# Item sums in 8 local slots per tile and a third picked tile in a message-passing kernel

## The reference

```python
v = edge_attr * (KS - 1); lo = jnp.floor(v); f = v - lo        # KS = 4, three dimensions
idx = jnp.clip(lo[:, None, :] + bits[None], 0, KS - 1)         # 8 corners of 64 = 4*4*4 cells
basis = jnp.prod(jnp.where(bits[None] == 1, f[:, None, :], 1.0 - f[:, None, :]), axis=-1)
wi = idx[..., 0] + KS * idx[..., 1] + KS * KS * idx[..., 2]
z = jnp.einsum('nc,kco->nko', x, W)                            # W is 64 x 32 x 32
msg = sum over the 8 corners s of basis[:, s, None] * z[src, wi[:, s]]
agg = segment_sum(msg, dst) / clip(count of dst, 1)[:, None]
return agg + x @ R + b
```

## Time and profile before

| | us |
|---|---|
| median of 3 runs | 20,975.38 |
| lowest, highest | 20,951.05, 21,013.64 |
| span of the profiled execution | 20,957.9 |
| TensorE busy (share of the span) | 15,299.0 (73%) |
| VectorE busy | 11,387.0 (54%) |
| GpSimd busy | 11,380.3 (54%) |
| ScalarE busy | 3,304.1 (16%) |

### The profile page before, as it was taken

The page is one execution under the profiler, slowest core; times in us unless marked ns, Lnnn a source line. Parts: engine busy times, 40 slices in busy tenths (PEclk is TensorE's granted clock), DMA queues, the critical chain, the costliest instruction groups (busy, mean ns, idle before and its releaser), DMA issues.

```text
span 20957.9 us, 179979 instructions
## 1 busy us (share of the span) xinstructions
PE 15299.0 (73%) x55111; PEld 8212.8 (39%) x55111; DVE 11387.0 (54%) x19145; ACT 3304.1 (16%) x4009; POOL 11380.3 (54%) x12003
## 2 busy tenths in 40 slices
PE   7788888888866767676666676667666676766676
PEld 3333333333333444443433343444443343434343
DVE  4556666656655555555545555555555555555555
ACT  1111111111111111111111111111111111111111
POOL 5445555555545555555545555555554555555554
PEclk7666666666678888888878888888887888888888
DMA  1000000000010000000010000000001000000000
GB/s 33 13 14 15 15 15 15 15 14 15 15 24 16 16 16 16 16 16 16 16 23 16 17 16 16 16 16 16 17 16 23 16 16 16 16 16 16 16 16 22
DMA packets 886190, 353.06 MB, mean 17 GB/s; under 512 B 604191, under 2 KB 877680, under 8 KB 885872
## 3 DMA queue, kind: packets, MB, share of 16 engines
q0 software_dynamic: 386208, 210.78, 5.9%
q1 hardware_dynamic: 329276, 112.29, 2.3%
q10 hardware_dynamic: 170644, 29.29, 0.8%
HBM read 314.88 MB, written 36.56 MB: 17 GB/s over the span
## 4 chain that ended last, share of the span: by engine, by line
PE 51%; another core or an unknown queue 28%; issue 14%; ACT 3%; DVE 3%; ACTq 1%; DMA 0%; POOL 0%; DVEq 0%; SPq 0%; POOLq 0%
PE ps L1547 17%; PE ps L1559 16%; PE ps L1459 5%; PE ps L1570 4%; PE ps L1475 3%; ACT big L792 2%; PE ps L1448 2%; PE ps L1442 2%; DVE big L1056 1%; PE ps L1432 1%; ACT big L710 1%; ACTq L802 1%; ACT big L700 0%; PE ps L1414 0%
## 5 line engine op out<-in xcount | busy, mean ns | idle before, releaser
L571 POOL DMA_INDIRECT xg<-x_rows,idx x8790 | 8316.4, 946 | 6310.6 <-DVE big L1254 3682.7
L1547 PE MATMUL ps<-big 128*128 128x256 f32 x18816 | 5050.5, 422 | 1286.7 <-ACT big L792 1250.4
L1237 DVE TENSOR_TENSOR big<-ps,onehot 128x1024 f32<-128x1024 f32 x2352 | 2864.7, 1218 | 5084.9 <-remote 3417.8
L1547 PEld LDWEIGHTS ps<-big 128*128 128x128 f32 x18816 | 3863.2, 211 | 3111.9 <-issue 2581.3
L571 POOL DMA_INDIRECT xg<-in_x,idx x3125 | 2974.6, 952 | 2806.5 <-DVE big L1026 1826.0
L1570 PE MATMUL ps<-big,w_taps 128*32 128x512 f32 x9408 | 1544.9, 734 | 3060.8 <-issue 2851.8
L792 ACT COPY big<-ps 128x1024 f32<-128x1024 f32 x2352 | 2353.5, 1013 | 8828.4 <-PE ps L1547 5318.7
L1559 PE MATMUL ps<-xw,big 128*128 128x512 f32 x8232 | 3671.5, 597 | 50.5 <-issue 23.2
L1459 PE MATMUL ps<-w,big 65*128 65x256 f32 x6272 | 2498.1, 541 | 126.9 <-DVE big L1056 85.6
L1559 PEld LDWEIGHTS ps<-xw,big 128*128 128x128 f32 x8232 | 1543.4, 190 | 2006.9 <-issue 1981.1
L1459 PEld LDWEIGHTS ps<-w,big 65*128 65x128 f32 x6272 | 1566.0, 267 | 1875.0 <-issue 1562.7
(11 more groups left out here) (139 smaller groups left out, 6620.8 us busy)
## 6 DMA issues: line engine op xcount, KB each, us to landing
xg<-x_rows,idx POOLq DMA_INDIRECT x8790
xg<-in_x,idx POOLq DMA_INDIRECT x3125
row_of<-pick_rows SPq DMA_DIRECT2D x294, 128.0 KB
agg_rows<-rts ACTq DMA_DIRECT2D x294, 64.0 KB
meta<-in_coord_t SPq DMA_DIRECT2D x294, 48.0 KB
big<-in_rad SPq DMA_DIRECT2D x196, 64.0 KB
meta<-meta_items SPq DMA_DIRECT2D x392, 32.0 KB
idx<-in_src_t SPq DMA_DIRECT2D x392, 16.0 KB
```

The source lines that it names most:

```text
L571: return nc.gpsimd.indirect_dma_start(out=dst_tile, out_offset=None, in_=table, in_offset=bass.IndirectOffsetOnAxis(ap=index, axis=0))
L1237: v.tensor_tensor(bm[:, ring], hat_outer[:, its].rearrange("p n c b -> p n (c b)").unsqueeze(3) .to_broadcast([P, 4, 16, J]), onehot[:, it ...
L1547: tr = nc.tensor.matmul(ps[:, 2 * (ch % 2) + r // 2, 256 * (r % 2):256 * (r % 2) + 256], xm[:, at].rearrange("p a c -> p (a c)"), bm[:, at ...
```

## The change

In the narrow path of the three layers a tile now has LOCAL = 8 local slots, which begin at its first destination rounded down to an even number (PAIR = 2). The widest tile of these inputs reaches place 7 there; the branch to the wide path now asks for 8 or more. Item sums have 128 columns instead of 256, taps 256 instead of 512, and `S` and `onehot` are half as wide. A chunk is 8 tiles, so a step has 4 chunks, one per group; `bm` and `xm` are rings of four such chunks, which is a whole step. GpSimd's group q waits for `xm_ready[q]`.

The frames of the scan are those of before (16 slots from a multiple of 8). So before the scan VectorE shifts each tile's 8 sums to their place in the frame: a one-hot of the shift (0, 2, 4 or 6), a product with it into four shifted copies (`spread`, whose other slots stay zero), and a sum over these (`in_pairs_to_frame`). The scan then reads `summed` in SBUF, not `ps`. It stands after the second of four chunks, before after the third of eight. The shift comes with `carry` as a second row.

PICKS = (1, 2, 3): the last tile of three groups is picked, so GpSimd has 29 gathers in groups of 8, 7, 7 and 7. The nodes of the seventh block of `xw` are 212, so that a short product (64 columns, L1659) with a table of their own, `tail`, takes the place of the seventh wide one; SyncE loads `tail` once per layer. The places come ready from a table, so `slot` (L1204) is dropped in the narrow path.

The diff, cut to its core (the tables' preparation and the wide path's side are left out):

```diff
+LOCAL = 8
+PAIR = 2
+SHIFTS = HALF // PAIR
...
-PICKS = (1, 3)
+PICKS = (1,2,3)
...
+        def layer_of(path):
+
+            tiles = 4 * J // path.slots
+            S, at = part(0, (2, 16, STEP, path.slots))
+            bm, at = part(at, (4, tiles, 16, path.slots))
+            xm, at = part(at, (4, tiles, GROUP, CH))
...
-                            else lambda q: (xm_ready[2 * q + 1], l * STEPS + i - 1))
+                            else lambda q: (xm_ready[(q + 1) * chunks // 4 - 1], l * STEPS + i - 1))
...
+            def in_pairs_to_frame(par, at):
+
+                v.tensor_tensor(layer.hot_shift, carry[:, par, 1].unsqueeze(1).to_broadcast([P, SHIFTS, STEP]),
+                                slot_ids[:, 0:SHIFTS].unsqueeze(2).to_broadcast([P, SHIFTS, STEP]), ALU.is_equal
+                                ).then_inc(dve_step, 1)
+                dve.wait_ge(dve_step, at + 1)
+                v.tensor_tensor(layer.spread[:, :, 0:LOCAL, :],
+                                ps[:, 7, 0:LOCAL * STEP].rearrange("p (s i) -> p s i", s=LOCAL).unsqueeze(1)
+                                .to_broadcast([P, SHIFTS, LOCAL, STEP]),
+                                layer.hot_shift.unsqueeze(2).to_broadcast([P, SHIFTS, LOCAL, STEP]), ALU.mult
+                                ).then_inc(dve_step, 1)
+                dve.wait_ge(dve_step, at + 2)
+                reach = (J - PAIR) * STEP
+                v.tensor_reduce(layer.summed.rearrange("p s i -> p (s i)")[:, 0:reach],
+                                layer.spread.rearrange("p d s i -> p (d s i)")[:, 0:SHIFTS * reach]
+                                .rearrange("p (d x) -> p x d", d=SHIFTS), AX.X, ALU.add).then_inc(dve_step, 1)
...
-                for ch in range(8):
-                    its = slice(4 * ch, 4 * ch + 4)
-                    ring = slice(4 * (ch % 4), 4 * (ch % 4) + 4)
-
-                    if due(8 * n1 + ch - 3):
-                        dve.wait_ge(s_done[ch % 4], 2 * n1 + ch // 4)
+                tiles = layer.tiles
+                for ch in range(layer.chunks):
+                    its = slice(tiles * ch, tiles * ch + tiles)
+                    q, last_of = (tiles * ch) // QUART, (tiles * (ch + 1)) % QUART == 0
+
+                    if due(layer.chunks * n1 + ch - 3):
+                        dve.wait_ge(s_done[ch % 4], each * n1 + ch // 4)
...
-                    if ch == 2 and with_scan:
-                        scan(n - 2, prior + LINKS1, P, l + 1, par, twice - 2)
+                    if ch == SCAN_AT and with_scan:
+                        scan(n - 2, prior + 7, P, l + 1, par, twice - 2)
...
-                for r in range(4):
-                    at = 4 * (ch % 4) + r
-                    tr = nc.tensor.matmul(ps[:, 2 * (ch % 2) + r // 2, 256 * (r % 2):256 * (r % 2) + 256],
-                                          xm[:, at].rearrange("p a c -> p (a c)"),
-                                          bm[:, at].rearrange("p k s -> p (k s)"), start=True, stop=True)
+                for r in range(tiles):
+                    at = wide * (r % (tiles // 2))
+                    tr = nc.tensor.matmul(ps[:, 2 * (ch % 2) + r // (tiles // 2), at:at + wide],
+                                          layer.xm[:, ch % 4, r].rearrange("p a c -> p (a c)"),
+                                          layer.bm[:, ch % 4, r].rearrange("p k s -> p (k s)"), start=True, stop=True)
...
-                for b in range(WB):
-                    tr = nc.tensor.matmul(ps[:, 6, :], row_hot[:, k, b, :], xw[:, b, :], start=(b == 0),
-                                          stop=(b == WB - 1))
-                tr.then_inc(pick_done, 1)
+                if k == 0:
+                    pe.wait_ge(pick_in, 48 + 16 * (l + 1))
+                for b in range(WB - 1):
+                    nc.tensor.matmul(ps[:, 6, :], row_hot[:, k, b, :], xw[:, b, :], start=(b == 0),
+                                     stop=False)
+                nc.tensor.matmul(ps[:, 6, 0:TAIL * CH], row_hot[:, k, WB - 1, :], tail[:], start=False,
+                                 stop=True).then_inc(pick_done, 1)
```

More of the change, by code:

```diff
@@ L49 @@
 BANK = 512
-Path = namedtuple("Path", "narrow items steps blocks picks")
+Path = namedtuple("Path", "narrow items steps blocks picks slots")
 def sizes(nodes, edges):
@@ L78, in graph_kernel @@
     LAYERS = 3
+    FULL = (WB - 1) * P * J
+    TAIL = 1
+    while TAIL * P < nodes - FULL:
+        TAIL *= 2
     ds = bass.ds
@@ L780, in scalar_program @@
                 nc.scalar.copy(x1[:, b, :], xw[:, b, :]).then_inc(x1_ready, 1)
+            layer = layer_of(path)
             def l1_step(l, i, par, with_rows):
[L784 to L785 removed]
+                n, each = layer.tiles, layer.chunks // 4
+                for ch in range(layer.chunks):
+                    if ch == layer.chunks // 2 and with_rows:
                         l1_rows(l, i - 2)
@@ L1184, in vector_program @@
             link(v.reciprocal(rcnt[:], rcnt[:]))
-            LINKS1 = 8
+            SCAN_AT = 1 if path.narrow else 2
+            LINKS1 = 7 if path.narrow else 8
+            each = layer.chunks // 4
+            row_hot, picked = layer.row_hot, layer.picked
             def l1_step(l, i, par, twice, prior, with_scan):
@@ L1262, in vector_program @@
                 link(v.tensor_copy(rows_ps, window_ids[:]))
+                if path.narrow and l == 0:
+                    link(v.memset(layer.spread, 0.0))
+                    link(v.memset(layer.summed, 0.0))
                 base1 = steps[0]
-                per1 = LINKS1 + SCAN
+                per1 = LINKS1 + SCAN + SPREAD
                 for b in range(WB):
```

234 lines of the change are left out of this document (142 added, 92 removed).

## The result

| | before | after |
|---|---|---|
| median, us | 20,979.92 (4 runs) | 21,892.85 (4 runs) |
| lowest to highest | 20,951.05 to 21,013.64 | 21,810.04 to 21,945.05 |
| ratio, 95% interval | | 1.0438, 1.0409 to 1.0467 |
| span of the profiled execution | 20,957.9 | 21,922.1 |

The change is 4.4% slower; the forecast was 5% faster, and the time lies above its own range (to 20,370 us) and above the wider one (to 21,100). The page's chain has changed its shares: what stood under "an unknown queue" has mostly become "issue", time in which an engine waits for nothing that the profile shows.

The account below looks back on a forecast made before the run. GpSimd's gathers plus idle from late-seen TensorE completions bound a step: 36.2 + 7.8 + 2.0 = 46.0 us for 49.75; -3.75 x 288 = -1080, -15 elsewhere, gives 19,880 us. Own range 19,450 to 20,370, wider 19,000 to 21,100.

Parts of the forecast that it names:

- Chains, groups, pauses: GpSimd: 29 gathers a step in chains of 22 and 7, with idle about 8 and 2 us.
- Work of the engines: TensorE's work a step 26 us for 31, VectorE net +1.0 on 26.0 busy; gathers 36.2 us.
- the reduction: VectorE's sum of 1792 values before the scan: 1.9 to 3.6 us, taken as 2.7.
- The next first pick ends at 25.4, 13.9 us into group 2's chain: held: TensorE finishes this pick during the 22 gathers; VectorE sees its completion only after them, 4.07 us past the end.
- the 7.8 forecast: GpSimd's idle behind 22 gathers: 4.07 us of late release, first pick 1.73, `xm` 1.22, 0.8 to GpSimd.
- The sum of the range: The step's own range from the reduction, the tail and the cold pick: 44.5 to 47.7 us.
- the tail: Time from the last gather of a long chain to TensorE's completions becoming visible: 4.07 us, range 3.3 to 4.8.
- the cold pick: TensorE's second pick, slow after the release, may last 10 us instead of 5.35; +0.8 us in the range.
- Rival A: The third pick is also held beside a chain: two holds at full price, 51.8 us a step, 21,550 us; chance 0.14.
- hold: TensorE's completions become visible late while a long chain of gathers runs, the last 4.07 us after it.
- Rival C: Completions were late only from crowded ScalarE or TensorE queues; halved work frees them: 37.5 us a step, 17,430 us; chance 0.06.

Follow-up runs that it names:

- e4: The changed kernel with one gather per group in the layers, 4 a step instead of 29, results not the reference's: 16,027.2 us, ratio 0.7633.
- e5: The changed kernel with 8 of TensorE's 16 taps products moved behind the next step's first pick and first chunk: 20,411.0 us, ratio 0.9800 to the kernel before.
- e2: The kernel before with the third pick alone added, 16 slots and chunks of 4 tiles kept: 20,098.9 us, ratio 0.9575.
- e13: The changed kernel word for word, in a comparison without holds: 15,037.5 us against 15,372.7 for the kernel before.

## Why the prediction was wrong

- *Chains, groups, pauses.* Right: 22 and 7, pauses of 1.8 for 2.0 us, the long idle before the first pick, none before `bm`.
- *Work of the engines.* Right in size: item sums 16 records in 2.05 us (what the forecast counts as 64 products are the two records each of 32), a pick 5.6 (5.35 forecast), the reduction 3.26 (2.7), VectorE 28.2 us busy a step for 27.0 forecast, and none of it is the bound (e4: 32.9 us).
- *"The next first pick ends at 25.4, 13.9 us into group 2's chain: held".* This step failed. It took TensorE to work on through a chain, with only its completions seen late. In fact its records come 1.5 to 2.8 us apart once a chain of this kernel is some 10 us old, and the taps were first in its queue. So all records of the pick but one came after the chain, and its 12 wide ones, 5.3 to 5.4 us elsewhere in the step, took 9.4 us here and 7.5 in the next step, at granted clocks of 0.68 and 0.69. The idle is 14.7 us in the mean for the 7.8 forecast, +7 x 288 = 2,000 us, the distance from 19,880 to 21,893. e5 puts the pick ahead of the taps, and the mean idle is 8.2.
- *What misled.* In the step I read, completions are late but TensorE doesn't creep. It executes 24 records in three runs without a break, 18 to 25 us into the chain of 22, behind a wait for ScalarE's late copy; VectorE needed none of them. None of the 281 chains of 22 in the kernel before has the creeping, so that no row of it could have priced it. A premise that holds under the old kernel's load was carried to a new load. TensorE executes 56 records in a chain there (median, at most 69); in a chain of the changed kernel it has executed 61 when the creeping begins, with more to do. The three runs of records:

```profile
12040.58 1.93 PE L1570 MATMUL ps<-big,w_taps 128*32 128x512 f32 x8 [7.07 <-ACT rts L799]
12042.44 3.45 PE L1547 MATMUL ps<-big 128*128 128x256 f32 x8
12045.83 1.07 PE L1570 MATMUL ps<-big,w_taps 128*32 128x512 f32 x8
```

- *The sum of the range.* The reduction (+0.9), the tail (+0.7) and the cold pick (+0.8) add up to 48.4 us a step, not 47.7; at 20,570 us this doesn't reach the result either.
- *Rival A* had the direction and nearly the time (21,550), not the mechanism: there is one hold a step. Its premise, that the added pick makes the loss, fell with e2. *Rival C*, no holds, isn't what this change brings, but e13 shows such a run, 36.4 us a step for the 37.5 worked out; what switches the holds off is not the lighter queues, for the kernel before has none there either. Its 17,430 us left out that the first layer is held as well: 58.9 us a step with holds and 40.7 in e13, 1,800 us.
- The Trainium skill (TensorE: Matmul & The Clock Gate, "The cost: per-tile semaphore tail") gives a model of the time from a matmul's end to its semaphore increment; for one tile and one increment an estimate by it is 0.056 us. e13 agrees, 0.04 us; the runs with holds do not: 20.1 us in the step that I read of the kernel before.
